# Masked attention: the mask added on the TensorE as four 64x64 tiles, for every part

## The reference

```python
def _L1_xattn_ref(values, keys, query, mask, heads, Wv, Wk, Wq, Wo, bo):
    ...
    energy = jnp.einsum('nqhd,nkhd->nhqk', q, k)
    energy = jnp.where(mask == 0, jnp.float32(-1e+20), energy)
    attn = jax.nn.softmax(energy / jnp.sqrt(jnp.float32(embed)), axis=3)
    out = jnp.einsum('nhql,nlhd->nqhd', attn, v).reshape(n, q_len, embed)
    out = out @ Wo.T + bo
    return out
```

## Time and profile before

| | |
|---|---|
| median of 3 runs | 3878.18 us |
| lowest and highest | 3874.96, 3878.55 us |
| span of the profiled execution | 3869.9 us |
| its own busy time of PE / DVE / ACT / POOL | 3678.2 / 3088.5 / 2207.4 / 2200.5 us |
| TensorE clock granted from 2482 to 3152 us | 1.00 of full |

### The profile page before, as it was taken

How to read it: one execution, slowest core, us unless ns; L and a number is a source line. 1 busy time by engine, 2 the same in 40 slices (tenths; PEclk the granted TensorE clock), 3 DMA queues, 4 the chain that set the end, 5 groups by cost and what they waited for, 6 DMA issues and landing times. The chain is left out here.

```text
span 3869.9 us, 134428 instructions
## 1 busy us (share of the span) xinstructions
PE 3678.2 (95%) x47408; PEld 2870.0 (74%) x47408; DVE 3088.5 (80%) x5266; ACT 2207.4 (57%) x4529; POOL 2200.5 (57%) x3316
## 2 busy tenths in 40 slices
PE   5999999995799999999999996999999999999999
PEld 4777777773688888888888884566666668888888
DVE  4888888885778777778777775798888977777777
ACT  3777777775444444444444442577677765555554
POOL 5666666664245443333333334466666667887777
PEclk9999999997899999999999998899999999999999
DMA  4677777774332322222222224799999952232322
GB/s 130 197 204 207 214 209 209 205 213 154 102 85 79 84 68 74 66 70 69 68 72 68 72 66 90 158 211 216 211 217 208 215 151 80 75 77 75 79 75 72
DMA packets 834241, 502.59 MB, mean 130 GB/s; under 512 B 262037, under 2 KB 824408, under 8 KB 833480
## 3 DMA queue, kind: packets, MB, share of 16 engines
q1 hardware_dynamic: 832680, 493.49, 50.5%
q0 software_dynamic: 928, 0.49, 0.1%
HBM read 251.27 MB, written 214.96 MB: 120 GB/s over the span
## 5 line engine op out<-in xcount | busy, mean ns | idle before, releaser
L1556 ACT ACTIVATE phase_spare<-phase_loop_hid,phase_b1T 128x128 f32<-128x128 f32 x2048 | 586.1, 368 | 710.9 <-PE phase_loop_hid L193 702.2
L1129 DVE TENSOR_REDUCE phase_loop_mx<-phase_loop_score 128x8 f32<-128x1024 f32 x512 | 625.4, 1222 | 98.5 <-PE phase_loop_score L882 91.0
L1522 PE MATMUL phase_loop_moe_y<-phase_w,phase_spare 128*128 x2048 | 693.6, 379 | 0.1
L1037 ACT ACTIVATE phase_loop_pt<-phase_loop_scoreT 128x1024 f32<-128x1024 f32 x448 | 458.6, 1024 | 268.3 <-PE phase_loop_scoreT L916 265.8
L1524 PE MATMUL phase_loop_moe_y<-phase_w,phase_spare 128*128 x2048 | 558.2, 273 | 0.0
L191 PE MATMUL phase_loop_hid<-phase_loop_moe_h,all_w_first_hi 128*128 128x128 f16 x2048 | 449.2, 219 | 0.0
L192 PE MATMUL phase_loop_hid<-phase_loop_moe_h,all_w_first_hi 128*128 128x128 f16 x2048 | 449.1, 219 | 0.0
L192 PE MATMUL phase_loop_hid<-phase_loop_moe_h,phase_w_hi 128*128 128x128 f16 x2048 | 449.1, 219 | 0.0
L193 PE MATMUL phase_loop_hid<-phase_loop_moe_h,all_w_first_lo 128*128 128x128 f16 x2048 | 449.1, 219 | 0.0
L193 PE MATMUL phase_loop_hid<-phase_loop_moe_h,phase_w_lo 128*128 128x128 f16 x2048 | 449.1, 219 | 0.0
L191 PE MATMUL phase_loop_hid<-phase_loop_moe_h,phase_w_hi 128*128 128x128 f16 x2048 | 449.0, 219 | 0.0
(11 more groups left out here) (293 smaller groups left out, 11038.9 us busy)
## 6 DMA issues: line engine op xcount, KB each, us to landing
qk_scratch<-phase_loop_qk SPq DMA_DIRECT2D x192, 256.0 KB, 3.4
phase_loop_cin<-in_ctx SPq DMA_DIRECT2D x128, 256.0 KB, 4.6
x_scratch<-phase_loop_x SPq DMA_DIRECT2D x128, 256.0 KB, 3.1
h_scratch<-phase_loop_hr SPq DMA_DIRECT2D x128, 256.0 KB, 3.7
phase_loop_qS<-qk_scratch SPq DMA_DIRECT2D x384, 64.0 KB, 2.8
phase_loop_kS<-qk_scratch SPq DMA_DIRECT2D x384, 64.0 KB, 2.4
ks_scratch<-ct_scratch SPq DMA_DIRECT2D x384, 64.0 KB, 2.4
all_w_first_lo<-ks_scratch SPq DMA_DIRECT2D x128, 192.0 KB, 4.0
```

Of the source, the lines that this page charges most:

```text
L1037: act.activation(pt[n % len(pt)][:, :, :], score_t_bank[:, :].rearrange("p (j n) -> p j n", j=HB2), ACT.Exp, scale=exp_scale).then_inc(s_e ...
L1129: v.tensor_reduce(to, score_bank[:, :].rearrange("p (h j n) -> p h j n", h=2, j=CH), AX.X, ALU.max).then_inc(s_mx.sem, 1)
L1522: pe.matmul(o[:, :], hh[n % NH][:, j, :], row, start=half == 0 and j == 0, stop=False, skip_group_check=True)
L1556: i = act.activation(hf[n % NF][:, j, :], hid(u, n)[:, j * S:(j + 1) * S], ACT.Gelu, bias=w["b1"][:, bass.ds(e * HB + (4 * half + j), 1)], ...
```

## The change

A mask product becomes four, of 64x64 tiles of the array. The tile at rows i and columns i carries half i of the mask to half i of the output in bank 0. For bank 1 the tile at rows i and columns 1 - i is used, with a second mask (`mask_x`, `maskT_x`) whose two halves of 64 rows are exchanged. All four parts are masked this way in both banks; the cut on DVE, the one on POOL, the ReLU and the second exponential are gone. The second masks are made by four DMAs of POOL's queue in the preparation, which waits for them.

```diff
+                def mask_tiles(bank, rows, crossed):
+
+                    for b, part in enumerate((rows, crossed)):
+                        for i in range(2):
+                            k_at, out_at = slice(64 * i, 64 * i + 64), slice(64 * (i ^ b), 64 * (i ^ b) + 64)
+                            pe.matmul(bank[out_at, b * 512:(b + 1) * 512], c["identb"][k_at, k_at], part[k_at, :],
+                                      start=True, stop=False, skip_group_check=True)
+
                 def mask_score(n):
 
                     def go(u):
                         s_mx.wait(pe, u, n)
-                        for hh in range(2):
-                            pe.matmul(score_bank[:, hh * 512:(hh + 1) * 512], c["identb"][:, :], w["mask"][:, :], start=True,
-                                      stop=False, skip_group_check=True)
+                        mask_tiles(score_bank, w["mask"], w["mask_x"])
                     return go
...
                     def go(u):
                         s_e.wait(pe, u, n)
-                        for hh in range(2):
-                            pe.matmul(score_t_bank[:, hh * 512:(hh + 1) * 512], c["identb"][:, :], w["maskT"][:, :],
-                                      start=True, stop=False, skip_group_check=True)
+                        mask_tiles(score_t_bank, w["maskT"], w["maskT_x"])
                     return go
...
-                    tasks = [(11, rows1), (4, maxima), (5, ctx_as_v), (6, cut(p, 3)), (9, rstd1)]
+                    tasks = [(11, rows1), (4, maxima), (5, ctx_as_v), (9, rstd1)]
...
-                             (7, copy_y(1)), (10, norm1), (6, expo(3)), (6, expo_under(3)), (8, hi_y)]
+                             (7, copy_y(1)), (10, norm1), (6, expo(3)), (8, hi_y)]
...
-                             (4, row_max(1)), (8, norm_y(1)), (2, lo_q), (4, row_max(2)), (6, cut(v, 1)),
+                             (4, row_max(1)), (8, norm_y(1)), (2, lo_q), (4, row_max(2)),
...
+        def cross(to, given):
+
+            g.dma_start(to[0:64, :], given[64:128, :]).then_inc(s_cross, 16)
+            g.dma_start(to[64:128, :], given[0:64, :]).then_inc(s_cross, 16)
+        g.wait_ge(s_v, 1 + CH)
+        cross(w["mask_x"], w["mask"])
+        g.wait_ge(s_turned, CH)
+        cross(w["maskT_x"], w["maskT"])
+        g.wait_ge(s_cross, 64)
...
-        v.tensor_scalar(w["keep"][:, :], b4[:, 0:S // 2].bitcast(BF16), 0.0, None, ALU.is_equal)
-        v.tensor_scalar(w["keep_min"][:, :], b4[:, 0:S // 2].bitcast(BF16), 0.0, KEPT, ALU.is_equal, ALU.mult)
+            v.tensor_copy(w["maskT"][:, j * S:(j + 1) * S], b4[:, 0:S // 2].bitcast(BF16)).then_inc(s_turned, 1)
```

More of the change, by code:

```diff
@@ L542, in attention @@
         s_y2, s_yh, s_yl, s_o, s_x1 = (g(n) for n in "s_y2 s_yh s_yl s_o s_x1".split())
-        s_cut, s_x = ({n: g(f"s_{what}{n}") for n in cut_by} for what in ("cut", "under"))
         s_xb, s_hrh, s_hr = g("s_xb"), g("s_hrh"), g("s_hr")
@@ L575, in heads @@
             return a, slice(a * S, (a + 1) * S), [4 * g4 + j for j in range(CH)]
[L577 to L589, removed]
         def ahead_of(u, count):
@@ L905, in score_t @@
                     a, at, blocks = heads(n)
-                    alone = first or n in cut_by
+                    alone = first
                     def go(u):
@@ L933, in go @@
                     def go(u):
[L934 to L937, removed]
+                        s_e.wait(pe, u, n + 1)
                         if n == 0 and u.static and u.no == 0:
@@ L982, in _ @@
                     tasks = [(6, av(0)), (3, score(0)), (8, make["t_y"]), (5, mask_score_t(0)), (4, make["t_max"]),
-                             (5, score_t(0)), (3, mask_score(1)), (6, av(1)), (3, score(1)), (5, score_t(1)),
+                             (5, score_t(0)), (3, mask_score(1)), (6, av(1)), (3, score(1)), (5, mask_score_t(1)), (5, score_t(1)),
                              (1, make["q"]), (7, make["y1"]), (3, mask_score(2)), (5, mask_score_t(2)), (3, score(2)),
                              (6, av(2)), (5, score_t(2)), (6, av(3)), (3, mask_score(3)), (6, make["y0"]),
-                             (3, score(3)), (5, score_t(3)), (8, make["o"]), (2, mask_score(0))]
+                             (3, score(3)), (5, mask_score_t(3)), (5, score_t(3)), (8, make["o"]), (2, mask_score(0))]
                 run_steps(pe, tasks, units, DEPTH, **follow("tensor", pe))
@@ L1032, in go @@
                         s_av.wait(act, u, n + 1 - len(pt))
-                        if n in cut_by and n in CUT_BY_PRODUCT:
-                            act.activation(pt[n][:, :, :], score_t_bank[:, :].rearrange("p (j n) -> p j n", j=HB2),
-                                           ACT.Relu, scale=-exp_scale).then_inc(s_e.sem, 1)
-                            return
                         act.activation(pt[n % len(pt)][:, :, :], score_t_bank[:, :].rearrange("p (j n) -> p j n", j=HB2),
                                        ACT.Exp, scale=exp_scale).then_inc(s_e.sem, 1)
-                    return go
-                def expo_under(n):
-                    def go(u):
-                        s_e.wait(act, u, n + 1)
-                        act.activation(pt[n][:, :, :], pt[n][:, :, :], ACT.Exp, scale=-1.0).then_inc(s_x[n].sem, 1)
                     return go
@@ L1672, in prepare_shared_heads @@
     b1, b2, b3, b4 = (kk.ps(f"sh_ps{i}") for i in range(4))
-    s_z, s_ld, s_mk, s_pe, s_v, s_a, s_row = (kk.sem(f"sh_{x}") for x in ("z", "ld", "mk", "pe", "v", "a", "row"))
+    s_z, s_ld, s_mk, s_pe, s_v, s_a, s_row, s_turned, s_cross = (
+        kk.sem(f"sh_{x}") for x in ("z", "ld", "mk", "pe", "v", "a", "row", "turned", "cross"))
     def gpsimd(g):
```

6 lines of the change are left out of this document (1 added, 5 removed).

## The result

| | before | changed |
|---|---|---|
| median of 4 runs each, same chip | 3876.57 us | 3899.76 us |
| lowest and highest | 3874.58, 3878.55 | 3897.93, 3900.53 |
| span of the profiled execution | 3869.9 | 3898.7 |

The ratio is 1.0060, with a 95% interval from 1.0047 to 1.0073: the change makes the kernel 23 us, 0.6%, slower. A second set of runs of the same two kernels gave 3893.28 against 3878.77 us, 1.0045 (1.0028 to 1.0062). So the loss is between 15 and 23 us by the medians; the forecast was 3876 and no change. (A ratio is worked out from all runs of both kernels, so it can differ a little from the ratio of the two medians.)

What follows compares the result with a forecast made beforehand. The PE was taken as the bound. Rounds +1.3, filling -3 and preparation -0.4 summed to -2 us, giving 3876; the mechanism's own range was 3858 to 3892, the stated range 3856 to 3922.

Steps and rivals of the forecast that it cites:

- Waits that could appear: PE's waits before transposed mask 1 (margin 0.04) and mask 1; less DVE, POOL and ACT work only widens margins.
- the forecast (+0.02): Phase three's round: PE instructions cost 0.08 us more, one wait of 0.06 goes; +0.02 a round, +1.3 us in 64.
- 0.1 to 0.2 a round: Errors of about 0.01 in fourteen division changes and eight tile products may add with one sign: 6 to 14 us.
- A single mask product: In the PE's round: four tiles at once take 0.23 us, or 0.325 with a change of division behind.
- A change of division: On the PE, each change into or out of 64x64 tiles costs 0.09 or 0.10 us, taken as 0.095.
- rival 2: Each of eight mask products runs tiles two at a time: 3986 us, chance 0.10; in three steps 4096, chance 0.04.
- Rival 4: Changes between tiled forms in the PE's round are nearly free: -0.86 us a round, 3821 us; chance 0.05.
- Rival 3: Changes into 64x64 tiles cost 0.12 to 0.15 us, fourteen times a round: 3898 to 3925 us; chance 0.10.
- The ends: Filling of phase three gets faster by an estimated 3 us, from 0 to 5; running out 0, with 2 either way.
- the preparation's -0.4: The DVE, last to finish the preparation, loses two passes of 0.28 us, overlapped to 0.4: -0.4 us.
- Rival 5: The DMA is the bound, so nothing changes but waits at score_t(0): 3876 to 3880 us; chance 0.02.
- Rounds can't become much shorter without new waits: Phase three's steady stretch: DMA share 0.99 taken as load, not as the round's limit; no size given.

Runs made afterwards that it cites:

- the maxima sooner: SyncE's list has place_max ahead of store_q and load_r; on the kernel before, with nothing else changed, 3872.15 us, ratio 0.9990.
- rounds of 11.17 us: Changed kernel with copy_y(0) ahead of hi_q, row_max(2) ahead of lo_q, and part 3 cut by POOL as before: 3886.12 us, ratio 1.0029.
- the kernel with rounds of 12.6: Changed kernel with each mask product as two whole-array products again, all four parts still masked: 3932.52 us, ratio 1.0150.
- both moves: Changed kernel with copy_y(0) ahead of hi_q on ACT and row_max(2) ahead of lo_q on the DVE, taking both waits out: 3887.61 us, ratio 1.0042.
- the loads moved too: Against the 3873.49 us kernel, four loads of next-stage weights moved from the end of SyncE's round to right behind store_max: 3870.95 us, 0.9987.
- masks 3 together: Changed kernel with both moves, plus y0 ahead of mask 3 so that mask 3 and transposed mask 3 stand together: 3892.97 us, ratio 1.0049.

## Why the prediction was wrong

**The step that failed** is "Waits that could appear". It looked at mask products that wait for `expo` and `row_max(0)`, and said of the work taken off DVE, ACT and POOL: "that only widens margins". It never asked what `av(2)` and mask 3 wait for. They came to wait 0.174 + 0.067 = 0.241 us a round, 61% of the 0.395 by which the round (+0.415) missed the forecast (+0.02). Taking both out gave back 0.247. The trace of before would have priced the first: a slack of 0.21 before `av(2)`, on a way that the forecast's own terms made shorter by twice as much in masks 2.

**The sizes.** The rest, 0.154 a round, is small errors of one sign, as the text had feared ("0.1 to 0.2 a round").
- A single mask product took 0.340 to 0.343, not 0.325; masks 2 together took 0.558, as forecast (0.555). With the neighbours, the six single products make +0.10.
- A change of division took 0.093 wherever it was new (`o` 1.320 to 1.414, `t_y` 0.493 to 0.585, scores 0.234 to 0.327): forecast 0.095. Of this the Trainium skill ("TensorEngine Tiling (Array Packing)", "Key Properties") says that changing the tiling mode drains the TensorE; the trace agrees in that each change costs time, and gives the price.
- `y0` behind mask 3 took 0.589, not 0.533, because its first f32 transpose took 0.165 in place of 0.109: +0.056. The forecast had no term for it, though the kernel before shows it: `t_y`, which follows `score(0)` across a change of division, has the same 0.165 for its first transpose, and so took 0.49 with no change behind it, where the forecast's own reading of four passes gives 0.44.

**Right:** four tiles at once, so rivals 2 (3986, 4096) fell at the first row. The Trainium skill's rule behind rival 2 (same page, "Gotcha 1: PSUM Pressure") does not hold here as a cost: row tiles that share a bank on different partitions took the same 0.340 as tiles that don't. Rival 4 fell by the 0.093. Rival 3 had nearly the right time (3898) by the wrong way: changes are 0.093, not 0.12. The measured 3899.8 lies outside the mechanism's own range (3858 to 3892) and inside the stated one (3856 to 3922) only through the room made for this rival, which is luck. The wait for `row_max(1)` went, and no idle stands before transposed mask 1 (2708.26 to 2708.58). DVE's share fell to 0.73 and POOL's to 0.42.

**The ends.** From the first `q` product to the first `t_y` the phase filled in 71.4 us (71.6 in the second trace of the changed kernel), where it took 72.4: -1.1, not -3. The kernel before with the maxima sooner took 71.6 as well, so even this can't be told from scatter. As it runs out, nothing changed (10.3 us from the last `t_y` to the first count in both). Phase two began 4.9 us later than before, at 995.4 in place of 990.6, but in the sixteen other runs with this preparation it began between 989.6 and 998.2: the preparation's -0.4 can't be told apart.

**Rival 5**, "nothing but waits at `score_t(0)`" with 0.02, was set too low. As a bound of the whole round it is wrong. But late rounds, which it stands for, are why rounds of 11.17 us gave no faster kernel, and why the kernel with rounds of 12.6 cost 7 to 12 us less than expected. "Rounds can't become much shorter without new waits" was right, and should have had its price.

The loss adds up: 57 rounds at +0.415 are 23.7 us, late time +1.0, filling -1.1, in the first set; with the late time of the second (7.7) it is 16, where 15 was measured.

## What to carry to other kernels

A step of the bounding engine that gets shorter brings that engine sooner to everything behind it. So for each of its instructions behind the edit, ask which end on which other engine it needs, what stands ahead of that in that engine's list, and how much slack there is from the moment that sets both off; not only for those that the diff names. Here a slack of 0.21 us stood on a way that got 0.37 shorter, and became the larger of the two waits. And when a list is mended, follow the task that is moved back to who waits for it: here `lo_q` held SyncE's queue, and through it the maxima.

No kernel found gains more than 0.13%. Masking part 1 by tiles, with POOL's cut of part 3, both moves and the maxima sooner, gave 3873.49 us, 0.9987 (0.9977 to 0.9997), and 3870.95, 0.9987, with the loads moved too. In the set of the first, the kernel before with nothing but the maxima sooner gave 3872.15, 0.9990. So it isn't shown that tiles have any part in that gain, and it is too small to matter.

## What the runs showed of the hardware

- Four 64x64 tiles start within 0.01 us of each other and stream 512 columns each in 0.24 us from one such product to the next; whole-array products took 0.43. All four products on the two tiles of one diagonal took 0.55 with a change behind them, where four tiles took 0.34.
- A change of the array's division cost 0.093 us, for 64x64 tiles as for rows and columns. The first f32 transpose behind one took 0.165 us in place of 0.109, before as after the change: behind scores (`t_y`), behind 64x64 tiles (`y0`), and behind `av(3)` in the kernel with masks 3 together.
- Two tiles of different row halves that wrote one bank on different partitions ran at once: 0.340 us for the product, as with no bank shared.
- Where it waited, the PE started 0.05 us after the DVE's end (2713.00 to 2713.05) and 0.15 after ACT's (2711.36 to 2711.51).
- The same kernel's late rounds differed by 7 us between two sets of runs, with each step of a normal round the same.
